# Where the output weights of layer 1 are sent and split, and in which order its first and last steps run

## The reference

```python
x = _layernorm(x + _L0_attn_ref(x, ...))
x = _layernorm(x + _L0_ffn_ref(x, gate_w, gate_up_proj, down_proj))
x = _layernorm(x + _L1_attn_ref(x, Wq, Wk, Wv, Wo, bo))
x = _layernorm(x + _L1_ffn_ref(x, weight, bias))
# layer 1, attention
q, k = _rope(q), _rope(k)
scores = 30.0 * jnp.tanh((scores + _alibi(t)) / math.sqrt(DQ) / 30.0)
probs = softmax(where(causal, scores, -inf))
out = (probs @ v).reshape(N, t, H * DV) @ Wo + bo
```

## Time and profile before

| | us |
|---|---|
| median of 3 runs | 571.01 |
| lowest, highest | 570.64, 573.57 |
| the profiled execution, whole | 576.58 |
| its span, from the first to the last instruction | 574.8 |
| PE busy in the span | 512.0 |
| DVE, ACT, POOL busy | 391.6, 337.9, 307.6 |

### The profile page before, as it was taken

One profiled execution on the slowest core, in us unless ns is written; L12 is line 12 of the kernel. 1 busy time (PEld: TensorE's weight loads), 2 busy tenths in 40 slices (PEclk: granted clock), 3 DMA queues, 4 the chain that ended last, 5 costly groups with the idle time before them and its releaser, 6 DMA issues.

```text
span 574.8 us, 10687 instructions
## 1 busy us (share of the span) xinstructions
PE 512.0 (89%) x3570; PEld 445.3 (77%) x3570; DVE 391.6 (68%) x840; ACT 337.9 (59%) x755; POOL 307.6 (54%) x300
## 2 busy tenths in 40 slices
PE   7988999999996994599993868999999999999892
PEld 6767888888875883486782858999999899999782
DVE  2579888888872356549763578778766986579453
ACT  4546767776776245055440486667766866686542
POOL 4746777767763035439762168665554644465210
PEclk9999999999999997789996798999999999999985
DMA  8929999800000912643535000000000000000001
GB/s 278 385 50 394 315 325 329 304 2 0 0 0 13 425 48 72 205 121 107 162 122 201 1 0 2 1 1 1 2 2 0 1 1 2 2 1 2 1 20 55
DMA packets 17581, 56.79 MB, mean 99 GB/s; under 512 B 2580, under 2 KB 12314, under 8 KB 15738
## 3 DMA queue, kind: packets, MB, share of 16 engines
q1 hardware_dynamic: 14784, 49.81, 25.4%
q0 software_dynamic: 2752, 6.40, 3.1%
HBM read 49.19 MB, written 28.45 MB: 135 GB/s over the span
## 4 chain that ended last, share of the span: by engine, by line
PE 72%; DVE 10%; ACT 5%; issue 5%; DMA 4%; POOL 3%; SPq 0%; ACTq 0%; DVEq 0%; POOLq 0%
PE bank L435 10%; PE bank L437 9%; PE bank L436 9%; PE bank L483 5%; PE bank L525 4%; PE bank L905 4%; PE bank L544 3%; PE bank L922 2%; PE bank L668 2%; PE bank L527 2%; PE bank L653 2%; PE bank L654 2%; PE bank L655 2%; PE bank L555 2%; PE bank L635 1%
## 5 line engine op out<-in xcount | busy, mean ns | idle before, releaser
L998 ACT ACTIVATE probs<-bank,neg_max,q_scale 128x256 f32<-128x256 f32 (+1 forms) x128 | 63.7, 507 | 39.4 <-DVE neg_max L1562 39.4
L1772 POOL TENSOR_TENSOR probs<-probs,inv_sum 128x512 f32<-128x512 f32 x64 | 51.6, 826 | 43.9 <-DVE inv_sum L1570 43.9
L1805 POOL TENSOR_TENSOR exps<-exps,tables 128x256 f32<-128x256 f32 x32 | 24.8, 776 | 77.9 <-ACT exps L1092 77.8
L1792 POOL TENSOR_TENSOR swapped<-swapped,tables 128x512 f32<-128x512 f32 x32 | 42.4, 1325 | 25.6 <-ACT swapped L1029 25.6
L1092 ACT ACTIVATE exps<-bank 128x768 f32<-128x768 f32 x32 | 25.9, 810 | 44.8 <-PE bank L635 44.8
L1404 DVE TENSOR_TENSOR q_lo<-q_sum,q_hi 128x512 fp32r<-128x512 f32 x32 | 27.2, 850 | 30.3 <-ACT q_hi L1062 30.2
L435 PE MATMUL bank<-x,wq_hi 128*128 128x256 f32 x128 | 39.3, 307 | 7.2 <-DVE q_sum L1391 7.2
L1548 DVE TENSOR_TENSOR swapped<-bank,tables 32x512 f32<-32x512 f32 x64 | 44.4, 693 | 1.4
L1908 POOL DMA_INDIRECT y_rows<-y_slot,dest x31 | 30.2, 973 | 27.3 <-DVE y_slot L1740 16.9
L1764 POOL TENSOR_TENSOR qT<-qT,swapped 128x512 f32<-128x512 f32 x32 | 40.8, 1275 | 7.1 <-DVE swapped L1548 7.1
L525 PE MATMUL bank<-keysT,qT 128*128 128x256 f32 x128 | 38.3, 381 | 0.7 <-ACT wo_full L1208 0.7
(11 more groups left out here) (264 smaller groups left out, 1817.4 us busy)
## 6 DMA issues: line engine op xcount, KB each, us to landing
slots<-in_c_unused SPq DMA_DIRECT2D x20, 1036.0 KB, 36.3
gu_all<-in_gate_up SPq DMA_DIRECT2D x4, 1024.0 KB, 7.9
xg<-slots SPq DMA_DIRECT2D x31, 129.5 KB
wvo_raw<-in_wvo SPq DMA_DIRECT2D x1, 2560.0 KB, 19.7
dn_all<-in_down SPq DMA_DIRECT2D x1, 2048.0 KB, 8.4
wq_full<-in_Wq SPq DMA_DIRECT2D x1, 2048.0 KB, 15.8
wo_raw<-in_Wo SPq DMA_DIRECT2D x1, 2048.0 KB, 11.4
yg<-y_rows SPq DMA_DIRECT2D x4, 512.0 KB, 5.4
```

Source lines behind the costliest of these rows:

```text
L998: ins = act.activation(probs[:, par, h, c0:c1], bank[:, 2 * par + h, c0:c1], ACT.Exp, bias=neg_max[:, par, i:i + 1], scale=q_scale[:, b, t ...
L1772: ins = pool.tensor_tensor(some, some, inv, ALU.mult)
L1792: pool.tensor_tensor(sw, sw, sin_rows(), ALU.mult).then_inc(at1["sin_done"], 1)
```

## The change

It moves work and adds or removes none. Four things are moved.

1. SP sends `Wo` behind the last block's rows instead of ahead of the first. ACT's eight high parts of it go from block steps 10 to 17 into units 0 to 7 of layer 1. POOL's eight low parts go from units 0 to 7 into units 1 to 8.
2. PE does the third group of queries right behind the first half of the values. The second half of the values of batch 0 goes into unit 0 and the second half of the keys into unit 1. ACT, DVE and POOL have the steps that belong to these keys one or two units later, and the swap of query group 2 earlier.
3. On ACT the root for batch 1 and the load of the tanh table go to the head of layer 1, ahead of the first swaps.
4. At the end `pe_ffn(2)` goes from unit 32 behind the last output product. On DVE `add_y(3)` and its statistics go ahead of `add_z(2)`, and `statistics(3, 2)` behind `normalise(2, 3)`. On ACT the root of batch 3 and its split go ahead of the last step of batch 2.

```diff
@@ PE, layer 1
         pe_values1(eng, 0, 0)
-        pe_keys1(eng, 0, 1)
-        pe_values1(eng, 0, 1)
         pe_queries1(eng, 2)
...
+            if n == 0:
+                pe_values1(eng, 0, 1)
+            if n == 1:
+                pe_keys1(eng, 0, 1)
...
-            if n == B * PAIRS:
-                pe_ffn(eng, 2)
             if n >= 3:
                 pe_out1(eng, n - 3)
+        pe_ffn(eng, 2)
         pe_turn_x(eng, 2, B - 1)
@@ ACT, layer 1
             if n == 0:
                 act_values(act, 0, 1)
+                act.wait_ge(ld["wo1_in"], 16)
+            if n == 1:
+                act_swap_keys(act, 0, 1)
+            if n == 2:
                 act_keys_hi(act, 0, 1)
+            if b == 0:
+                act.activation(heads_of(wo_hi, u), heads_of(wo1_raw, u), ACT.Copy).then_inc(kv["w_hi"], 1)
@@ DVE, layer 1
         query_cos(1)
         query_sum(1)
+        query_cos(2)
         query_lo(1)
-        keys_cos(0, 1)
-        query_cos(2)
         query_sum(2)
@@ POOL, layer 1
-        for m in range(2):
+        for m in range(3):
             sin_queries(m)
-        sin_keys(0, 1)
-        sin_queries(2)
...
-            if b == 0:
-                pool.wait_ge(kv["w_hi"], PAIRS + u + 1)
...
+            if 1 <= n <= PAIRS:
+                pool.wait_ge(kv["w_hi"], PAIRS + n)
...
+            if n == 1:
+                sin_keys(0, 1)
@@ SP
         sp.wait_ge(ln["y_done"], NT)
-        sp.dma_start(wo1_raw[:], a["Wo1"].rearrange("(h p) n -> p h n", p=P)).then_inc(ld["wo1_in"], 16)
         sp.wait_ge(ld["scattered"], 16 * NT * TOP)
...
+        sp.dma_start(wo1_raw[:], a["Wo1"].rearrange("(h p) n -> p h n", p=P)).then_inc(ld["wo1_in"], 16)
         for j in range(4):
             sp.wait_ge(y_out[j], 16 * len(range(j, STEPS, 4)))
```

More of the change, by code:

```diff
@@ L1074, in act_layer1 @@
         act_x_hi(act, 1, 0)
+        act_root(act, 1, 1)
+        load_table(act, 2 * B + 2, ACT.Tanh)
         act_swap_keys(act, 0, 0)
@@ L1077, in act_layer1 @@
         act_keys_hi(act, 0, 0)
+        act_swap_queries(act, 1)
         act_query_hi(act, 0)
-        act_swap_queries(act, 1)
-        act_root(act, 1, 1)
-        load_table(act, 2 * B + 2, ACT.Tanh)
-        act_query_hi(act, 1)
-        act_swap_keys(act, 0, 1)
         act_swap_queries(act, 2)
         act_values(act, 0, 0)
+        act_query_hi(act, 1)
         for n in range(B * PAIRS + 2):
@@ L1154, in act_layer1 @@
         act_last_step(act, 1)
+        act_root(act, 2, 3)
+        act_x_hi(act, 2, 3)
         act_root(act, 3, 2)
-        act_root(act, 2, 3)
         act_last_step(act, 2)
-        act_x_hi(act, 2, 3)
         act_root(act, 3, 3)
@@ L1245, in _ @@
                 act.activation(chunk(wq_hi, k - 2), chunk(wq_full, k - 2), ACT.Copy).then_inc(kv["w_hi"], 1)
-            if k == 2 + PAIRS:
-                act.wait_ge(ld["wo1_in"], 16)
-            if 2 + PAIRS <= k < 2 + 2 * PAIRS:
-                act.activation(heads_of(wo_hi, k - 2 - PAIRS), heads_of(wo1_raw, k - 2 - PAIRS),
-                               ACT.Copy).then_inc(kv["w_hi"], 1)
         load_table(act, 2 * B + 8, ACT.Sqrt)
@@ L1445, in dve_layer1 @@
             b, u = divmod(n, PAIRS)
-            if n == 0:
+            if n == 2:
                 keys_sum(0, 1)
@@ L1468, in dve_layer1 @@
             if n == 0:
+                normalise(1, 1)
+            if n == 1:
+                keys_cos(0, 1)
+            if n == 2:
                 keys_lo(0, 1)
-                normalise(1, 1)
             if 1 <= b < B - 1 and u == 0:
@@ L1512, in dve_layer1 @@
                 x_lo(2, 2)
-        add_z(2)
         shift_of(1)
-        statistics(3, 2)
         add_y(3)
         statistics(2, 3)
+        add_z(2)
         normalise(2, 3)
+        statistics(3, 2)
+        x_lo(2, 3)
         shift_of(2)
-        x_lo(2, 3)
         add_z(3)
```

7 lines of the change are left out of this document (4 added, 3 removed).

## The result

| | before | changed |
|---|---|---|
| median of 9 runs each, us | 572.02 | 567.72 |
| lowest, highest | 569.56, 575.54 | 564.63, 569.48 |
| profiled execution, us | 576.58 | 566.75 |
| its span, us | 574.8 | 564.9 |

The ratio is 0.9917, with a 95% interval of 0.9888 to 0.9946: 0.8% faster, some 4.7 us. The direction was right. The forecast time, 560.6, and its range, 557.0 to 565.5, were not: the median lies 2.2 us above the range. Three later comparisons of the same two kernels gave 0.9863, 0.9915 and 0.9892. Weighted by their intervals, all four give 0.9903 +- 0.0018, which is 5.5 us +- 1.0. The gain is real and about half of the forecast.

What follows compares the result with a forecast made beforehand. TensorE, busy 512.0 of 574.8 us, was taken as the bound, with gains only where it idles or runs at half clock. Terms 4.7 + 0.8 - 0.5 + 4.0 + 1.4 = 10.4 off 571.0 gave 560.6 us, range 557.0 to 565.5.

Steps and rivals of the forecast that it cites:

- (a): Rival, ahead of the experts: the scatter was held by its place behind the others, not by Wo; 566.1 us, chance 0.10.
- (c): Rival, end of the experts: Wo holds up the scatters and the rows fetched back; slower, 571.5 us, chance 0.02.
- (b): Rival, head of layer 1: its waits turn into new ones, only 0.5 of 4.0 us is left; 564.1 us, chance 0.10.
- (d): Rival: the clock stays full after the scatter and in the first units; another 2.5 us, 558.1 us, chance 0.10.
- the walk: Head of layer 1: new lists followed by the rows' durations; TensorE's idle times fall from 6.8 to 3.3 us.
- The scatter, 4.7: Ahead of the experts: without Wo the last token scatter lands in 2.5 us instead of 7.17, gaining 4.7 us.
- The clock behind it, 0.8: At the first expert blocks: a slow-clock stretch of 3.3 us in place of 5.2 gives back 0.8 us.
- Wo beside the last expert scatters, -0.5: Last expert blocks: scatters running beside Wo come somewhat late, costing 0.5 us, with bounds 0 and 2.6.
- The head, 4.0: Head of layer 1: the new order gains 3.5 us of idle time plus part of a slow-clock stretch, 4.0 us together.
- The wait at the second turned context: Layer 1, unit 2: POOL's four instructions in unit 1 delay the mask, so TensorE waits 1.7 to 2.0 us.
- The end, 1.4: End of the kernel: the linear layer of batch 2 leaves the line and add_y comes earlier; 1.4 us gained.
- The third term: End of the kernel: x's split on ACT no longer waits behind the last step of batch 2; 0.4 us gained.

Runs made afterwards that it cites:

- `after_again`: The changed kernel run again without edits; ratio 0.9863 to the kernel before.
- `pieces`: The changed kernel with Wo sent in eight pieces of 256 KB behind the rows of blocks 12 to 19; 563.75 us, ratio 0.9842 to the kernel before.
- `wo_rows_back`: The changed kernel with Wo sent even later, behind the rows fetched back; 567.50 us, ratio 0.9849 to the kernel before.
- `low_later`: The changed kernel with POOL's eight low parts of Wo in units 2 to 9, not 1 to 8; 569.54 us, ratio 0.9873 to the kernel before.
- either part alone: Two runs on the kernel before: only item 1 of the change, ratio 0.9961; only items 2 and 3, ratio 0.9971.
- `before_third`: The kernel before run again unchanged, on the same chip as a repeat of the changed kernel; ratio 1.0006 to the kernel before.
- `after_third`: The changed kernel run again without edits, on the same chip as `before_third`; ratio 0.9915 to the kernel before.
- `b_again`: The kernel before run again unchanged; ratio 1.0018, its traced execution 572.70 us.
- `before_fill`: The kernel before with filler matmuls, 76 ahead of the wait for the rows fetched back and 34 behind (18 before); ratio 1.0053.

## Why the prediction was wrong, point by point

Most mechanisms were the predicted ones, each at its place. None of the rivals took place as a whole: (a) and (c) are excluded by the landings of 3.30 and 2.41 us, (b) by the stage to scores 8, and (d) by the times. Of (d)'s picture the slow stretch behind the third wait is indeed gone in all four traces, but one stands at the first keys or the first scores instead (315.0 to 322.2 us), and the clock at the first blocks is full in `after_again` alone. What failed were sizes, two waits that the walk missed, and the way from one trace to a median. The range had a fault of its own: it ends at 565.5, below the prediction's own number for rival (a), 566.1.

**The scatter, 4.7.** Right in cause: without Wo it lands in 3.30, 3.04, 3.04 and 2.92 us in the four traces. Wrong in size: the step that failed is "so without Wo I take 2.5". The landing gained 4.0 us (7.0 less 3.1 in the mean), and like against like the first turned block comes 3.8 us earlier. The scatters of 226 to 229 us, from which the 2.5 is, lie further ahead in the run; why the last two take longer even without Wo (3.5 and 3.3 us in the changed kernel) isn't shown.

**The clock behind it, 0.8.** The stage gained 0.9 in the mean, but the four single values are 0.5, 1.5, 0.8 and 0.9 against the mean of before. Right in the mean.

**Wo beside the last expert scatters, -0.5.** The traces show -0.9, and -1.1 with the stage behind it. The step "At 7.3 us plus about 0.5 ... it would be 1.3 us late; at half of the delay it would be in time. I take -0.5" chose the mild half. One buffer was 1.4 us late at POOL, which is the prediction's own 1.3, and most of that stayed. `pieces` and `wo_rows_back` show the cause: with 256 KB at a time, or with Wo sent later, nothing is late.

**The blocks between.** Leaving out the one stop of 2.4 us, they cost 0.3 us more. The prediction had nothing there.

**The head, 4.0.** 3.6 us up to scores 8, and 0.2 given back in the units behind, where ACT and POOL now do the Wo splits: 3.4. The walk met its starts: it had query group 3 start 14.7 us behind the turn of x (330.6 - 315.86), and it started 15.0 behind it (327.04 - 312.08). But the step "After, by the walk: ... together 3.3. That leaves 3.5 us" failed. Up to scores 8 the idle times of TensorE of over 0.2 us, without that of 1.46 us at the first keys, sum to 6.8, 6.8 and 7.0 us in the three traces of before and to 5.0, 4.2, 4.7 and 4.2 in the four of the changed kernel. That is 2.4 us less in the mean, not 3.5. What it missed are 1.8 us ahead of query group 2 in two traces, and up to 1.5 us ahead of the first scores, where it had 0.7. Its own sign, group 3 within 4.2 us of group 2, was not met either: 5.1, 5.4, 6.1 and 5.4.

The other 1.2 us of this stage go with the clock: inside it TensorE worked 9.9, 9.9 and 3.9 us at its lower level in the traces of before, and 2.9, 3.4, 6.6 and 3.4 in those of the changed kernel. In two of the three traces of before the lower clock behind the experts still holds over the first keys and queries (up to 323.8 us in the first). With Wo moved it has ended by then in every trace, though in some a new, shorter stretch begins there. In the kernels with Wo at its old place and no filler four of five traces have it. That speaks for a tie to Wo's place, which the prediction doesn't have; what ties them isn't shown.

The wait at the second turned context was found with its size. Its cause was half right. POOL's row of work is in the chain, but the last link is DVE's add in front of c_lo, which a low part of Wo on POOL holds up by some 1.0 us (an estimate from the rows under `low_later`). The same wait stands in kernels with either part alone.

**The end, 1.4.** 0.7. From scores 31 to the last `add_y` it gained 0.97, not 1.3 (15.66 us in `before_third`, 14.69 in the changed kernel), from there to the turn it lost 0.25, as forecast. The third term, "that is gone" (0.4), did not come: from the turn to the last linear layer it is 2.74 us after 2.69. POOL's and DVE's timelines:

```profile
553.43 1.17 POOL L1816 TENSOR_TENSOR x_rows<-x_rows,tables 128x512 f32<-128x512 f32 x1 [11.66 <-PE bank L443]
```

```profile
553.15 0.30 DVE L1292 BATCH_NORM_AGGREGATE moments<-bn_out 128x2 f32<-128x6 f32 x2
553.48 1.14 DVE L1294 TENSOR_SCALAR var_eps<-moments 128x2 f32<-128x2 f32 x1
554.54 0.68 DVE L1358 TENSOR_TENSOR x<-bank,x 128x512 fp32r<-128x512 f32 x1
```

`statistics(3, 2)` now stands ahead of x's low part. Its last step (`var_eps`, on 128x2 elements) took 1.14 us instead of 0.17, while the high part was ready at 553.9. The rows show what held it: POOL's add on x, L1816, started 0.05 us ahead of it, and DVE's step ended as POOL's did, at 554.6. The same holds over all 18 traces: the 240 of these steps that start while POOL does no arithmetic take 0.17 us, and the 48 that start beside it end 0.02 to 0.06 us behind POOL's instruction. So ACT's wait was exchanged for one of DVE on POOL. With this step behind x's low part the forecast 0.4 might come; no run tests that.

So the terms of the sum were worth 3.8 + 0.9 - 0.3 - 1.1 + 3.4 + 0.7 = 7.4 us, not 10.4. That is 3.0 of the 7.1 us between 560.6 and 567.72.

**The base, 1.0.** I took the gain off 571.0, the median of three runs. Nine runs in the comparison gave 572.02.

**The rest, 3.1, is open; the clock and chance are argued, not shown.** The first comparison showed a gain of 4.3 between its medians, where the terms are worth 7.4; all four together show 5.5 +- 1.0, so 1.9 stay. Two things point at how it could close. The four profiled executions of the changed kernel are on average 0.6 us shorter than the medians of their comparisons. And executions differ by stretches at the lower clock. The one in layer 0's attention is an example (first `after_third`, then `after_again`):

```profile
178.00:185.00 7.00, 5.58 (x26) 4.02 (x27) 0.00 (x0) 2.64 (x5) 0.94 (x2) 0.56 0.12 22
```

```profile
178.00:185.00 7.00, 3.96 (x29) 3.11 (x30) 0.26 (x3) 4.03 (x10) 1.61 (x2) 1.00 0.10 19
```

At 6.8 us of length it costs 2.3 to 2.7 us, as said. It is in three of the four traces of the changed kernel and in one of the three of before, and in all traces taken, in 7 of 11 of kernels built on the changed one (in two of them shorter, in two longer) and in 1 of 7 of the others. No engine's list differs up to there. Whether that is chance or a real cost of the change, about 1 us, stays open.

**The profiled execution of before.** It lay 5.6 us above the median, and the prediction took all of that off as a constant. For the largest part that was right: 3.3 us lay ahead of the first attention matmul (39.9 us; 36.6 and 37.1 in the other two). Its slow stretches at 347.7 and 545.7 us were not rare: `b_again`, with 572.70 us close to the median, has both, `before_third` has neither. The prediction counted only 0.5 us of the first and nothing of the second, so they are not what made the sum too large. Together with the start they made the two profiled executions lie as far apart as forecast.

What the Trainium skill, "DMA: Bandwidth & Descriptors", section "Queues, rings and completion order", says of whole packets taken from one ring at a time fits what it was used for: the one known scatter of the last six beside 2 MB on the other queue took 6.1 us, those beside pieces of 256 KB 2.8 in the median. No run here shows single packets.

## What to carry to other kernels

A large transfer on one queue can delay small ones on another while it lasts: look at whose scatters or fetches run beside it. Here 2 MB behind the last fetch cost the last blocks 0.9 us. Sent still later, or in eight pieces of 256 KB between the blocks, it cost them nothing. Before a stretch at the lower clock is priced as a gain, look whether a second trace of the same kernel has it: here two of three had it, and filling TensorE's gap did not hold the clock. When a profiled execution is 1% above the median, a second trace, cut at the same events, tells in which stages the excess sits. And when DVE instructions are moved, look at what POOL does at the new place: two of the waits here are DVE instructions that ended only when a POOL instruction did.

## What the hardware showed that I had not expected

TensorE's clock fell to its lower level for 3.3 us in a stretch in which it worked without pause, though it had been busy for 12.57 of 14 us at the full level shortly before (`before_fill`). Slow stretches differ between executions of one kernel in place and in number, and go with most of the spread of 569 to 577 us. A DVE instruction on 128x2 elements took 1.14 us instead of 0.17 in all twelve traces with the new order of the end, because a POOL instruction had started 0.05 us ahead of it; the same one takes 0.94 to 0.96 at another place in every trace, again up to the end of a POOL instruction. The shortest medians are those of the kernels with Wo in eight pieces: `pieces` is 1.6% (1.2 to 2.0%) under the kernel before, and with the rows of bo later as well it is the same within the error, 1.4% (1.0 to 1.9%).
